# Norms, roundings and silu products moved to VectorE, the convolution's left tap split over ScalarE and GpSimd, and identity turns put into TensorE's queue

## Chip, cores and metric

One core of a Trainium2 chip. The metric is the device time of one execution in microseconds (us), the median of the runs shown; from run to run this kernel moves by under 1%.

## What is computed

Two layers over x of 2 examples x 512 tokens x 128 channels, with a context of 77 tokens per example. The reference, cut to what matters:

```python
# layer 0: cross attention in which the 512 tokens are the queries (8 heads of 64);
# its keys and values are the 512 tokens and the 77 context tokens together
q, k, v = heads(ln @ Wq), heads(kv @ Wk), heads(kv @ Wv)
x = x + tanh(g) * (softmax(q * 8 @ k.T) @ v) @ Wout
# layer 0: feed-forward on the layer norm of x, with quantised values and ternary weights
h = bit_linear(layernorm(x), w1)          # act_quant: round(x * 127 / max|x|) * max|x| / 127
h = silu(depthwise_conv1d(h, conv_w) + conv_b)     # three taps along the tokens, 512 channels
x = x + tanh(g) * bit_linear(h, w2)
# layer 1: attention to the 77 context tokens, 16 heads of 8, rotary factors on q and k
x = x + tanh(g) * attention(layernorm(x), ctx)
# layer 1: 8 experts of width 64, the two best per token, and a shared expert
y = x + tanh(g) * moe(layernorm(x))
```

## The kernel before, in words

Tokens lie on the 128 partitions in eight tiles, four for each example. The work is cut into items, each named by a kind and its indices, and each item passes several stages on several engines. The order in which every engine walks its items is written out by hand in the string PLAN, as words "kind:stage": F and B are TensorE's two visits, A1 and A2 ScalarE's, D0 to D3 VectorE's, P1 to P3 GpSimd's, Ca and Cd a copy out of PSUM by ScalarE or by VectorE; the number behind F is the PSUM bank that the item takes. Word by word the string is dealt out into one fixed list per engine, so each engine works strictly in its own list's order, and items meet through semaphores. An F item first waits until the former holder of its bank has been read out.

The kinds that matter, in the order in which one example passes them:

- x0, q, k, v: normalised and transposed input, projections. u: one tile and head of attention: scores (lines 596, 597), maximum on VectorE (1012), exponential on ScalarE (823), five transposes back (551, the helper `turn`), one copy of 640 columns (772 ScalarE, 774 VectorE). w: for a pair of heads, weighted sum of the values (615), 16 in all. o: output projection (622) and new X1 with the statistics of its norm.
- n: the norm ahead of the quantised layer, in halves of two tiles. VectorE gives mean and variance (950, 951, 961); GpSimd raises the variance to the power -1/2 (462) and normalises two tiles (465); VectorE finds their largest magnitudes (1224 to 1226); GpSimd rounds by adding and subtracting a large constant MAGIC (533, 536). f1 transposes the tiles.
- f2: per chunk of 128 channels, four chunks: product with the ternary weights in two passes (639, 640); ScalarE makes the middle tap and the bias (859), VectorE adds the left tap (1063) and the right tap (1065), ScalarE takes tanh (917); the silu product (tanh + 1) * y of chunks 0 and 1 is GpSimd's (488, 489), of chunks 2 and 3 VectorE's (1166). TH is the tanh buffer, two deep.
- f3: four transposes per tile (551), VectorE's largest magnitude (1071 to 1074), ScalarE scales and adds MAGIC (870), GpSimd subtracts it and writes bf16 (494). f4: transposes (652), ScalarE's copy (875), product (733), new X2 (1171) and the next norm, again by halves: power and normalisation on GpSimd.
- a1: transposes of the norm; a2: queries (667) and their rotation on VectorE (1107, 1110); a4: eight items per example, each scores of eight heads (675), maximum and subtraction on VectorE (1115, 1118), exponential (881), transposes, copy (786 or 788); a6: weighted sums (687, 692), reciprocal and product on VectorE (1124, 1125), output projection (746), and the norm by halves.
- m1, m3, m2, m4: transposes, router and shared expert (702, then a chain of small VectorE steps, 1130 to 1199), experts' two products (709, 751), tanh, mixture products on GpSimd (515, 543), and the last projection (757, 758) and store.

The second example's attention (u, w) is mixed with the first one's later layers; after its last w nothing is left that could fill the gaps but the first example's experts.

Of the kernel before, what the change touches and what calls it, by code (L numbers as in the profile page):

```python
# [100 lines left out]
x0:F0 x0:A1 k:F0 k:F2 x0:D2 k:A1 q:F4 k:A1 k:D1 v:F6 q:A1 k:D1 s:D2 q:F5 v:Ca q:D1 v:F2 q:A1 q:D1 u:F6 v:Ca  # L101
u:F0 u:F2 u:D1 u:D1 v:F5 u:A1 u:D1 u:A1 u:B v:Cd u:A1 u:B u:Cd u:B u:Ca u:F6 u:Ca u:F0 u:D1 u:F2 u:D1 u:A1
k:F4 u:D1 u:A1 u:B w:D0 k:A1 w:P1 u:B u:Cd u:A1 u:Cd u:F6 u:B k:D1 u:F0 u:Cd u:F4 u:D1 q:F2 u:D1 u:A1 q:F3
u:D1 u:A1 u:B u:A1 u:B w:D0 u:Cd q:A1 u:B u:Cd s:F6 w:F7 s:D1 k:F0 w:P1 u:Ca q:D1 w:A1 w:F6 k:A1 w:D1 k:D1
u:F0 w:A1 w:D1 u:F4 u:D1 u:F6 u:D1 g:F2 u:A1 u:D1 u:A1 u:B g:D1 u:A1 u:B u:Cd u:B u:Ca w:D0 w:P1 u:F0 u:Ca
u:F4 u:D1 u:F6 u:D1 u:A1 w:F2 u:D1 u:A1 u:A1 u:B w:A1 w:D1 u:B u:Ca u:B u:Cd u:F0 u:Ca k:F4 u:D1 q:A1 k:F6
u:A1 q:D1 k:A1 u:B k:A1 u:Cd k:F2 w:D0 k:D1 w:P1 k:F0 k:A1 k:D1 u:F4 k:D1 k:A1 u:F6 u:D1 w:F2 u:D1 u:A1 k:D1
u:A1 u:B w:A1 w:D1 u:B u:Ca u:F2 u:Cd u:F4 u:D1 u:F6 u:D1 a3:F0 u:A1 u:D1 u:A1 u:B u:A1 w:D0 a3:D1 w:P1 u:B
u:Ca u:B u:Ca u:F2 u:Ca w:F4 u:D1 a3:P1 u:A1 u:B w:A1 w:D1 u:F6 u:Ca u:F4 u:D1 u:F2 u:D1 u:A1 x0:F0 u:D1
u:A1 u:B u:A1 u:B w:D0 u:Cd w:P1 x0:A1 u:B u:Cd u:F6 u:Ca u:F4 u:D1 q:F2 u:D1 u:A1 u:F0 u:A1 u:B u:D1 q:A1  # L110
u:B u:Cd w:F3 u:A1 u:Cd w:D0 q:D1 u:F4 w:P1 w:A1 w:D1 u:F6 u:D1 u:B u:D1 k:F2 u:A1 u:Cd u:A1 u:B k:A1 u:B
u:Cd u:F0 u:Ca k:D1 u:F4 u:D1 w:F2 u:D1 u:A1 u:A1 w:D0 u:B w:A1 w:P1 w:D1 u:B u:Ca o:F2 u:Cd o:F3 o:D1 k:F4
# [37 lines left out]
def takes(item, stage):  # L150

    kind, n = item[0], item[-1]
    return {"x0 D2": n == 0, "f2 P1": n < HC // 2, "f2 D2": n >= HC // 2, "f4 P2": n % TP == TP - 1}.get(f"{kind} {stage}", True)


def orders():
# [3 lines left out]
    for word in PLAN.split():  # L160
        kind, stage = word.split(":")
        engine = COPIER.get(stage) or ENGINE[stage[0]]
        if stage[0] == "F":
            stage, bank = "F", int(stage[1:])
        elif stage[0] == "C":
            stage = "C"
# [1134 lines left out]
```

## Time and profile before

| what | us |
| --- | --- |
| median of 3 runs | 305.68 (303.73 to 306.17) |
| the profiled execution, its own time | 305.48 |
| its span, first to last instruction | 303.7 |
| TensorE busy | 267.9 |
| VectorE busy | 221.0 |
| ScalarE busy | 167.9 |
| GpSimd busy | 90.8 |

The profile is one execution. PE is TensorE's matmuls and transposes, PEld its weight loads (they overlap), DVE VectorE, ACT ScalarE, POOL GpSimd; "granted clock" 1.00 is 2.4 GHz and 0.50 is 1.2 GHz. Some 1.8 us of a run lie outside the span.

### The profile page before, as it was taken

The numbers are of one execution on the slowest core, as the hardware profiler recorded it, in microseconds if no ns is written. First come the engines' busy times: TensorE is split into PE (matmuls) and PEld (weight loads), VectorE is DVE, ScalarE is ACT, GpSimd is POOL, SyncE is SP. The second block draws the span as 40 slices with busy tenths as digits, with TensorE's granted clock in tenths as the row PEclk, the third lists the DMA queues.
The fourth block names the chain that finished last, engine by engine and source line by source line (L and its number), as shares of the span: only waits on it lengthen the run. The fifth ranks groups of instructions, "written<-read, shape, count | busy, mean of one in ns | idle before, by whom it ended". The sixth has DMA issues, their size and how long they took to land.

```text
span 303.7 us, 5371 instructions
## 1 busy us (share of the span) xinstructions
PE 267.9 (88%) x1806; PEld 191.1 (63%) x1806; DVE 221.0 (73%) x501; ACT 167.9 (55%) x336; POOL 90.8 (30%) x116
## 2 busy tenths in 40 slices
PE   0899999999999989978999999999779568997786
PEld 0568677698777665756766687775358444654455
DVE  3698976786867689949888984588687747665671
ACT  1385557677562589756757676452564612451451
POOL 2100000010005607346010030045996780003571
PEclk9999999999999999999999999999997965579899
DMA  7930000000000000000000000000000100000001
GB/s 214 370 108 3 0 1 2 0 2 0 3 0 2 1 0 0 2 3 1 0 3 0 2 0 2 1 2 0 2 1 9 29 0 0 0 2 0 0 3 35
DMA packets 5855, 6.12 MB, mean 20 GB/s; under 512 B 555, under 2 KB 4805, under 8 KB 5829
## 3 DMA queue, kind: packets, MB, share of 16 engines
q1 hardware_dynamic: 4944, 4.66, 4.9%
q10 hardware_dynamic: 885, 1.12, 1.0%
q8 instruction: 15, 0.25, 0.3%
q14 instruction: 11, 0.09, 0.1%
HBM read 5.26 MB, written 0.52 MB: 19 GB/s over the span
## 4 chain that ended last, share of the span: by engine, by line
PE 62%; DVE 17%; POOL 9%; issue 6%; ACT 4%; DMA 1%; DVEq 0%; ACTq 0%; POOLq 0%
PE slot L551 18%; PE slot L615 10%; PE slot L596 5%; POOL XN L465 5%; PE slot L597 4%; PE slot L757 3%; PE slot L675 3%; PE slot L587 3%; POOL vex L462 2%; PE slot L580 2%; PE slot L574 2%; PE slot L588 2%; PE slot L667 2%; DVE nm L1012 2%; DVE aq L1071 1%
## 5 line engine op out<-in xcount | busy, mean ns | idle before, releaser
L823 ACT ACTIVATE PR<-slot,nm 128x589 f32<-128x589 f32 x64 | 47.7, 751 | 22.2 <-DVE nm L1012 22.0
L1012 DVE TENSOR_REDUCE nm<-slot 128x1 f32<-128x589 f32 x64 | 46.3, 763 | 8.4 <-PE slot L597 8.1
L551 PE MATMUL slot<-K,PR 128*128 128x128 f32 (+1 forms) x320 | 44.2, 279 | 1.7 <-ACT PR L823 1.4
L551 PEld LDWEIGHTS slot<-K,PR 128*128 128x128 f32 (+1 forms) x320 | 35.4, 142 | 14.0 <-ACT PR L823 9.7
L596 PE MATMUL slot<-KH,Q 128*128 128x296 f32 (+1 forms) x128 | 40.8, 337 | 1.3 <-ACT PT L786 0.6
L615 PE MATMUL slot<-PT,V 128*64 128x256 f32 (+1 forms) x320 | 38.1, 384 | 0.0
L597 PE MATMUL slot<-KL,Q 128*128 128x296 f32 (+1 forms) x128 | 36.1, 299 | 0.0
L462 POOL TENSOR_TENSOR vex<-vex,mhalf 128x2 f32<-128x2 f32 (+1 forms) x14 | 10.7, 762 | 83.5 <-DVE vex L961 83.4
L482 POOL COPY REC<-rec 128x256 f32<-128x256 f32 x16 | 6.5, 408 | 95.7 <-DVE rec L990 59.6
L772 ACT ACTIVATE PT<-slot 128x640 f32<-128x640 f32 x36 | 25.1, 705 | 8.9 <-PE slot L551 6.0
L615 PEld LDWEIGHTS slot<-PT,V 128*64 128x64 f32 (+1 forms) x320 | 21.5, 137 | 11.9 <-issue 2.7
L596 PEld LDWEIGHTS slot<-KH,Q 128*128 128x128 f32 x128 | 24.1, 188 | 6.5 <-issue 1.5
L774 DVE COPY PT<-slot 128x640 f32<-128x640 f32 x28 | 22.5, 820 | 3.9 <-PE slot L551 3.7
L597 PEld LDWEIGHTS slot<-KL,Q 128*128 128x128 f32 x128 | 24.2, 189 | 0.7 <-issue 0.7
L551 PE MATMUL slot<-K,XN 128*128 128x128 f32 x32 | 8.5, 333 | 13.3 <-DVE XN L964 7.6
L465 POOL TENSOR_SCALAR XN<-X,mvx,vex 128x128 f32<-128x128 f32 x24 | 19.0, 798 | 1.3
L881 ACT ACTIVATE S<-S 128x616 f32<-128x616 f32 x16 | 11.3, 715 | 13.7 <-DVE S L1118 13.6
L1019 DVE TENSOR_TENSOR OT<-slot,RB 128x256 f32<-128x256 f32 x16 | 6.7, 421 | 14.7 <-ACT RB L835 12.8
L1115 DVE TENSOR_REDUCE mx<-slot 128x8 f32<-128x616 f32 x16 | 12.7, 796 | 6.2 <-PE slot L675 6.2
L551 PEld LDWEIGHTS slot<-K,XN 128*128 128x128 f32 x32 | 4.7, 153 | 18.3 <-issue 11.9
L551 PE MATMUL slot<-K,S 128*128 128x128 f32 x80 | 13.9, 325 | 2.3 <-ACT S L881 2.3
L551 PEld LDWEIGHTS slot<-K,S 128*128 128x128 f32 x80 | 10.9, 166 | 7.2 <-ACT S L881 4.7
(163 smaller groups left out, 539.0 us busy)
## 6 DMA issues: line engine op xcount, KB each, us to landing
CTT<-in_ctxT SPq DMA_DIRECT2D x1, 640.0 KB, 8.1
K<-in_const ACTq DMA_DIRECT2D x1, 589.0 KB, 8.3
WGU<-in_wgu SPq DMA_DIRECT2D x1, 580.0 KB, 8.7
X<-in_x SPq DMA_DIRECT2D x2, 256.0 KB, 3.9
WK<-in_wk SPq DMA_DIRECT2D x1, 512.0 KB, 6.2
out<-X SPq DMA_DIRECT2D x8, 64.0 KB, 1.5
L1W<-in_l1w SPq DMA_DIRECT2D x1, 384.0 KB, 8.1
WD<-in_wdT SPq DMA_DIRECT2D x1, 320.0 KB, 9.6
```

The source lines that it names most:

```text
L462: return pool.tensor_tensor(vex[:, n, r], vex[:, n, r], mhalf[:, r], ALU.pow)
L465: return pool.tensor_scalar(XN[:, m, :], src[:, m, :], mvx[:, n, m, 0:1], vex[:, n, m:m + 1], ALU.subtract, ALU.mult)
L551: return pe.transpose(dst, src, ident[0:p, 0:p])
L596: pe.matmul(W[:, K0 + lo:K0 + hi], q, KH[:, g % 4, lo:hi], start=True, stop=False)
L597: mm = pe.matmul(W[:, K0 + lo:K0 + hi], q, KL[:, g % 4, lo:hi], start=False, stop=True)
L615: mm = pe.matmul(W[e * DH0:(e + 1) * DH0, 0:N], V[0:r, c, h * DH0:(h + 1) * DH0], PT[0:r, s, c, e, :], start=(c == 0), stop=(c == 4))
L772: engine.activation(dst, src, ACT.Copy).then_inc(pt_copied["ACT"], 1)
L774: engine.tensor_copy(dst, src).then_inc(pt_copied["DVE"], 1)
L823: act.activation(PR[:, s, :], W[:, K0:K0 + KEYS0], ACT.Exp, bias=nm0[:, s:s + 1], accum_out=sum0[:, b, p * 2 + f, t, e:e + 1]).then_inc(pr ...
L881: act.activation(s1, s1, ACT.Exp, scale=float(DH1) ** -0.5).then_inc(exp1_ready, 1)
L1012: dve.tensor_reduce(nm0[:, s:s + 1], W[:, K0:K0 + KEYS0], AX.X, ALU.max, negate=True).then_inc(max_ready, 1)
L1115: link(dve.tensor_reduce(mx, w, AX.X, ALU.max))
```

## The change

Four edits and a new PLAN of 894 words instead of 874.

1. Normalisations of halves (n, f4, a6) and the rounding of n go from GpSimd to VectorE (stage D3); GpSimd keeps the power -1/2. The subtraction of MAGIC in f3 goes from GpSimd to ScalarE (6 of 8 tiles, Ca) or VectorE (2, Cd).
2. All eight silu products are VectorE's.
3. Convolution: ScalarE writes the left tap into TH (new stage A3), ScalarE the middle tap and VectorE the right tap as before, and GpSimd adds TH, moved by one column, to the sum. Then tanh overwrites TH.
4. A word such as "f3:F5+7" lets TensorE turn the identity 7 times into the item's slot after the slot is free and before it waits for its data; there are 54 such turns: 7 in x0's neighbour q at the start, 20 from f3 to f4, 12 in a2 and a4, 15 in m1, m3 and m4, the last three groups all in the second example.

In the new PLAN ScalarE takes 44 of 64 u copies (36 before), 14 of 16 a4 copies (15) and 4 of 6 v copies (5). In the last part the lists read, shortened:

```
VectorE before  w:16 a6 o:7 o:8 m2 n(half 4) m3 m2 m3 m2 f1 m2 a3 f2 f2 f2 f2 ... f3 x4 f4 x4 a2 a2 a4 x8
VectorE after   w:16 m2 m2 o:7 o:8 n(half 4) m2 m2 f1 a3 f2 m4 f2 f2 f2 m4 f2 m4 f2 ... f3 x4 f4 x2 norm f4 x2 a2 norm a4 a4 a2 a4 x6
TensorE before  f4 ... a1 a2 a1 a2 a4 a4 a4
TensorE after   f4 ... a1 a2(+2) a4(+8) a4 a4 a1 a2(+2)
```

```diff
-        return {... "f2 P1": n < HC // 2, "f2 D2": n >= HC // 2, "f4 P2": n % TP == TP - 1}
+        return {... "f4 P2": n % TP == TP - 1, "f4 D3": n % TP == TP - 1}
...
                 elif kind == "f2":
                     c = item[2]
-                    pool.wait_ge(tanh_done, n)
-                    th = TH[:, (n - 1) % 2, :]
-                    link_all([pool.tensor_scalar(th, th, 1.0, None, ALU.add)])
-                    pool.tensor_tensor(YC[:, c, :], YC[:, c, :], th, ALU.mult).then_inc(silu_by_pool, 1)
-                elif kind == "f3":
-                    pool.wait_ge(rounded, n)
-                    if n > 2:
-                        pool.wait_ge(qbt_ready, n - 2)
-                    pool.tensor_scalar(QB[:, (n - 1) % 2, :], QM[(n - 1) % 2], MAGIC, None,
-                                       ALU.subtract).then_inc(qb_ready, 1)
+                    pool.wait_ge(conv_left, n)
+                    pool.wait_ge(conv_right, n)
+                    pool.tensor_tensor(YC[:, c, 1:S], YC[:, c, 1:S], TH[:, (n - 1) % 2, 0:S - 1],
+                                       ALU.add).then_inc(conv_done, 1)
...
+                for _ in range(WARM[item]):
+                    turn(W[:, 0:P], ident)
...
+        def copy_quantised(engine, by, item):
+            n = upto(item)
+            engine.wait_ge(rounded, n)
+            if n > 2:
+                engine.wait_ge(qbt_ready, n - 2)
+            dst, src = QB[:, (n - 1) % 2, :], QM[(n - 1) % 2]
+            if by == "ACT":
+                engine.activation(dst, src, ACT.Copy, bias=-MAGIC).then_inc(qb_copied["ACT"], 1)
+            else:
+                engine.tensor_scalar(dst, src, MAGIC, None, ALU.subtract).then_inc(qb_copied["DVE"], 1)
...
+            def third(item):
+                c, n = item[2], upto(item)
+                act.wait_ge(front_done, NTH[item] + 1)
+                if n > 2:
+                    act.wait_ge(silu_ready, n - 2)
+                if item[1] == 1 and c < 2:
+                    act.wait_ge(hidw_ready, QT)
+                act.activation(TH[:, (n - 1) % 2, :], slot(item)[:, 0:S], ACT.Copy,
+                               scale=cw[:, 3 * c:3 * c + 1]).then_inc(conv_left, 1)
...
-                    link(dve.scalar_tensor_tensor(out=y[:, 1:S], in0=W[:, 0:S - 1], scalar=cw[:, 3 * c:3 * c + 1],
-                                                  in1=y[:, 1:S], op0=ALU.mult, op1=ALU.add))
...
             def third(item):
-                link(dve.tensor_reduce(aq[:, r, 0], XN[:, r, :], AX.X, ALU.max, apply_absolute_value=True))
-                link(dve.tensor_scalar(aq[:, r, 3], aq[:, r, 0], 1e-5, 1.0 / 127, ALU.max, ALU.mult))
-                dve.reciprocal(aq[:, r, 2], aq[:, r, 3]).then_inc(quant_ready, 1)
+                kind, n = item[0], upto(item)
+                if kind == "n":
+                    dve.wait_ge(rstd_ready[1], n)
+                    link_all([dve.tensor_scalar(XN[:, m, :], X1[:, m, :], mvx[:, 1, m, 0:1], vex[:, 1, m:m + 1],
+                                                ALU.subtract, ALU.mult) for m in tiles])
+                    link(dve.tensor_reduce(aq[:, r, 0], XN[:, r, :], AX.X, ALU.max, apply_absolute_value=True))
+                    link(dve.tensor_scalar(aq[:, r, 3], aq[:, r, 0], 1e-5, 1.0 / 127, ALU.max, ALU.mult))
+                    link(dve.reciprocal(aq[:, r, 2], aq[:, r, 3]))
+                    link_all([dve.tensor_scalar(XN[:, m, :], XN[:, m, :], aq[:, m, 2:3], MAGIC,
+                                                ALU.mult, ALU.add) for m in tiles])
+                    for m in tiles:
+                        dve.tensor_scalar(XN[:, m, :], XN[:, m, :], MAGIC, aq[:, m, 3:4],
+                                          ALU.subtract, ALU.mult).then_inc(xn_ready[1], 1)
+                elif kind == "f4":
+                    dve.wait_ge(rstd_ready[2], n // TP)
+                    for m in range(n - TP, n):
+                        normalise(2, X2, m, XN[:, m, :], xn_ready[2])
+                elif kind == "a6":
+                    dve.wait_ge(rstd_ready[3], n)
+                    for m in range(part_tiles(item).start, part_tiles(item).stop):
+                        normalise(3, X3, m, XN[:, m, :], xn_ready[3])
```

## Rows read from the trace of the kernel before

**Rows 1.** The page: busy time of the engines, and the granted clock by slice.
```profile
PE 267.9 (88%) x1806; PEld 191.1 (63%) x1806; DVE 221.0 (73%) x501; ACT 167.9 (55%) x336; POOL 90.8 (30%) x116
...
PEclk9999999999999999999999999999997965579899
```

**Rows 2.** Busy time by stretch: window, its length, then each engine, clock, DMA.
```profile
20.00:204.00 184.00, 176.19 (x1301) 132.31 (x1299) 142.98 (x283) 120.01 (x248) 38.05 (x53) 1.00 0.01 1
...
204.00:222.00 18.00, 15.85 (x86) 9.37 (x82) 13.81 (x48) 6.13 (x13) 13.83 (x19) 1.00 0.00 1
222.00:234.30 12.30, 10.00 (x53) 8.00 (x53) 9.83 (x20) 7.53 (x15) 10.25 (x9) 0.86 0.02 6
234.30:253.60 19.30, 13.41 (x87) 9.64 (x88) 11.69 (x40) 6.61 (x12) 11.84 (x12) 0.79 0.04 11
253.60:270.90 17.30, 15.71 (x97) 8.51 (x95) 12.47 (x16) 8.09 (x12) 0.00 (x0) 0.55 0.00 1
270.90:284.20 13.30, 11.19 (x91) 7.07 (x84) 8.10 (x26) 4.29 (x9) 2.29 (x3) 0.87 0.00 0
```

**Rows 3.** The same view in stretches of 2 us, where the clock fell.
```profile
226.00:228.00 2.00, 0.11 (x1) 0.12 (x2) 1.97 (x4) 1.58 (x4) 1.59 (x3) 1.00 0.00 0
...
244.00:246.00 2.00, 0.84 (x5) 0.41 (x5) 1.71 (x7) 0.26 (x1) 1.88 (x3) 0.85 0.00 0
```

**Rows 4.** Groups of instructions by line and shape: busy us, mean ns | idle before.
```profile
L772 ACT ACTIVATE PT<-slot 128x640 f32<-128x640 f32 x36 | 25.1, 705 | 8.9 <-PE slot L551 6.0 <-PE slot L615 2.5
...
L465 POOL TENSOR_SCALAR XN<-X,mvx,vex 128x128 f32<-128x128 f32 x24 | 19.0, 798 | 1.3
...
L494 POOL TENSOR_SCALAR QB<-W 128x512 bf16<-128x512 f32 x8 | 11.8, 1492 | 8.0 <-ACT W L870 6.1 <-ACT QBT L875 1.8
...
L859 ACT ACTIVATE YC<-slot,COL,cw 128x512 f32<-128x512 f32 x8 | 5.8, 786 | 0.5 <-PE slot L640 0.5
L536 POOL TENSOR_SCALAR XN<-XN,aq 128x128 f32<-128x128 f32 x8 | 5.7, 720 | 0.4
...
L917 ACT ACTIVATE TH<-YC 128x512 f32<-128x512 f32 x8 | 5.1, 642 | 2.9 <-POOL YC L489 2.1 <-DVE YC L1065 0.8
...
L533 POOL TENSOR_SCALAR XN<-XN,aq 128x128 f32<-128x128 f32 x8 | 2.9, 371 | 2.9 <-DVE aq L1226 2.9
...
L964 DVE TENSOR_SCALAR XN<-X,mvx,vex 128x128 f32<-128x128 f32 x8 | 2.2, 342 | 1.5 <-POOL vex L462 1.5
...
L852 ACT ACTIVATE XH<-slot 128x512 fp32r<-128x512 f32 x2 | 1.2, 598 | 2.2 <-PE slot L551 2.2
```

**Rows 5.** Instructions in order of time, 234 to 282 us: start, us, instruction.
```profile
234.45 1.96 PE L551 MATMUL slot<-K,YC 128*128 128x128 f32 x16
...
237.17 5.97 POOL L494 TENSOR_SCALAR QB<-W 128x512 bf16<-128x512 f32 x4 [4.34 <-ACT W L870]
...
243.43 0.17 DVE L961 TENSOR_SCALAR vex<-mvx 128x2 f32<-128x2 f32 x1
...
250.16 2.04 PE L667 MATMUL slot<-LT,L1W 128*128 128x256 f32 x4 [0.52 <-ACT LT L877]
...
253.58 0.80 DVE L1115 TENSOR_REDUCE mx<-slot 128x8 f32<-128x616 f32 x1
254.41 0.80 DVE L1118 TENSOR_TENSOR S<-slot,mx 128x616 f32<-128x616 f32 x1
...
279.92 1.91 PE L709 MATMUL slot<-WGU,LT 128*128 128x512 f32 x2
...
281.62 1.06 PE L746 MATMUL slot<-L1W,A1T 128*128 128x128 f32 x4
```

**Rows 6.** In order of time around 215 us: a GpSimd product beside a VectorE step.
```profile
215.31 1.27 POOL L543 TENSOR_TENSOR HM<-HM,TH 128x512 f32<-128x512 f32 x1
...
215.84 0.77 DVE L1225 TENSOR_SCALAR aq<-aq 128x2 f32<-128x2 f32 x1
```

**Rows 7.** Busy time by stretch, in the first example's convolution.
```profile
110.00:120.00 10.00, 9.80 (x45) 6.27 (x45) 9.78 (x14) 9.95 (x20) 5.54 (x4) 1.00 0.00 0
```

More of the change, by code:

```diff
@@ L163, in orders @@
         if stage[0] == "F":
-            stage, bank = "F", int(stage[1:])
+            bank, turns = [int(n) for n in (stage[1:] + "+0").split("+")[:2]]
+            stage = "F"
         elif stage[0] == "C":
@@ L173, in orders @@
             mine = range(bank, bank + 1 + wide(item))
-            bank_of[item], had[item] = bank, list(dict.fromkeys(holder[i] for i in mine if i in holder))
+            bank_of[item], warm[item], had[item] = bank, turns, list(dict.fromkeys(holder[i] for i in mine if i in holder))
             holder.update({i: item for i in mine})
-    return order, bank_of, had, copier
-ORDER, BANK_OF, HAD, COPIES = orders()
+    return order, bank_of, had, copier, warm
+ORDER, BANK_OF, HAD, COPIES, WARM = orders()
 NTH = {x: n for n, x in enumerate(x for x, stage in ORDER["PE"] if stage == "F")}
@@ L402, in col, with quantised @@
             return COL[:, COLS.index(name):COLS.index(name) + 1]
-        def silu(item):
-            _, b, c = item
-            half = HC // 2
-            return (silu_by_pool, b * half + c + 1) if c < half else (silu_by_dve, b * half + c - half + 1)
+        def quantised(n):
+            item = KINDS["f3"][n - 1]
+            return qb_copied[COPIES[item]], copied(item, COPIES[item])
         def half_pair(item):
@@ L647, in front @@
                     n = upto(item)
-                    pe.wait_ge(qb_ready, n)
+                    pe.wait_ge(*quantised(n))
                     pe.wait_ge(identb_ready, 1)
@@ L868, in first @@
                     if n > 2:
[L869 removed]
+                        act.wait_ge(*quantised(n - 2))
                     act.activation(QM[(n - 1) % 2], W[:, 0:HID], ACT.Identity, bias=COL[:, NCOL - 1:NCOL],
@@ L921, in second @@
                     if n % QT == 1:
-                        for c in range(HC):
-                            act.wait_ge(*silu(("f2", item[1], c)))
+                        act.wait_ge(silu_ready, HC * (n // QT + 1))
                     if n > 2:
@@ L926, in second @@
                     act.activation(HB[:, (n - 1) % 2, :], slot(item)[:, 0:MH], ACT.Tanh, scale=0.5).then_inc(gate_tanh, 1)
+            def third(item):
[7 more added lines that the diff above has]
+                               scale=cw[:, 3 * c:3 * c + 1]).then_inc(conv_left, 1)
             def copy(item):
-                {"u": copy_turned, "a4": copy_turned1, "v": copy_values}[item[0]](act, "ACT", item)
-            walk("ACT", {"A1": first, "A2": second, "C": copy})
+                {"u": copy_turned, "a4": copy_turned1, "v": copy_values, "f3": copy_quantised}[item[0]](act, "ACT", item)
+            walk("ACT", {"A1": first, "A2": second, "A3": third, "C": copy})
         @block.vector
```

175 lines of the change are left out of this document (72 added, 103 removed).

## The prediction

> **What bounds the kernel now.** I read the page's busy line and slices first: TensorE is busy for 88% of the span, and its granted clock sinks only in the last third [rows 1]. So I cut the span at the places where the work changes, with a view that gives busy time by stretch [rows 2]. From 20 to 204 us, where attention of both examples runs with the later layers of the first one between, TensorE is busy 176.2 of 184 us at full clock. VectorE has 143 there, ScalarE 120, GpSimd 38. That stretch is near TensorE's, and at most 7.8 us of visible idle can go from it. From 204 us on, the last 100 us, no engine is full in most stretches: the second example's quantised layer, its second attention and its experts form one chain of short steps. What a step is worth is read from there, and that is where nearly all my terms lie.
>
> In that tail the clock falls from 2.4 to 1.2 GHz. It fell at 228 us, after 226 to 228 in which TensorE was busy for 0.11 us, and again inside 244 to 246, after a stretch of short turns with gaps [rows 3]. It then stayed down through nearly all of 253.6 to 270.9 (mean 0.55) although TensorE was busy 15.7 of 17.3 us there [rows 2]. So in that stretch TensorE is the bound only because of its clock.
>
> **The change, part by part**, against the profiled execution (305.48 us, span 303.7; the median of the runs is 0.2 above).
>
> Prices of the moved operations [rows 4]. A normalisation of a tile costs 0.80 us on GpSimd and 0.34 on VectorE; a half of two tiles takes 1.60 or 0.68. The second rounding step costs 0.72 a tile on GpSimd and on VectorE the same 0.34, since it has the same form. Subtracting the magic number from 512 columns costs 1.49 on GpSimd; no row shows it elsewhere. ScalarE's nearest row is a plain 512-column copy, 0.60, and the one with scale and bias from a tensor is 0.79; I take 0.60 to 0.70. The left tap on ScalarE lies between the same two rows; I take 0.70. GpSimd's sum of two 512-column operands has the form of its product, 1.27 [rows 6]. A turn of the identity is a turn like the 16 that took 1.96 us [rows 5], 0.12 each: 54 of them are 6.6 us of TensorE, 47 of them in the tail, all placed after the slot is free and before the wait for data. While TensorE would wait anyway they cost nothing; uncovered, all would cost 6.6.
>
> *20 to 204 us: -1.0.* GpSimd's latencies in the first example's quantised layer go, which should close about 2 of the 7.8 us idle. The new order puts a transposed half and a router product (0.9 us) ahead of the last weighted sum. The bounds are -5 and +5, since an order of 894 words is new throughout.
>
> *204 to 222 us (end of attention to the quantised layer): -2.0.* GpSimd is busy 13.8 of 18 us [rows 2]. The second half's normalisation gives 0.9, its rounding (now 0.68 + 0.68 for 2.17) 0.8. The power no longer queues behind another half's normalisation (0.5), and the second attention's reciprocal of the first example is out of the way of the last head pair (0.8). That is 3.0. Against it stands the following. A VectorE step on 128x2 elements took 0.77 us at 215.84 instead of 0.32 and ended when GpSimd's 1.27 us product, begun at 215.31, ended [rows 6]. The new tensor_scalars are of that kind, and the mixture products still run on GpSimd beside them: I charge 1.0, with 0 and 2.5 as ends.
>
> The Trainium skill has this as a rule (SBUF — State Buffer, "Who interferes with whom"): a VectorE tensor_scalar in a two-port mode, or one with two SBUF inputs against a reading GpSimd, is blocked until the other engine's instruction ends. The trace agrees in that one pair of rows. It speaks against the change in just this place: by it each of the three linked groups of a half could be blocked once.
>
> *222 to 234.3 us (convolution and silu): +1.2.* Before, GpSimd was busy for 10.25 of the 12.3 us, with half of the silu products and the last mixture products. The new chain for a chunk is longer: left tap, middle tap, right tap, GpSimd sum 1.27, tanh, product. ScalarE now does 4 x (0.70 + 0.79 + 0.64) = 8.5 us [rows 4] and all four expert outputs' copies, some 3.4, where it was busy 7.5 of 12.3 [rows 2]; it is near full. Since TH has two buffers, the third left tap waits for the first product. Followed, the last product ends 13.4 us after the first convolution product, where it was 12.2.
>
> *234.3 to 253.6 us (quantise, second linear layer, first queries): -4.3.* Before, GpSimd's four subtractions fill 237.17 to 243.14 [rows 5]. In their place ScalarE does 4 x 0.78 rounding, 3 x 0.6 subtraction and 4 x 0.60 copies, 7.3 us from about the same start, so the second half's variance hardly moves. But the first half's, at 243.43 before [rows 5], comes about 1.5 earlier, its normalisation is 0.9 shorter, and its query product runs at full clock (-1.0). The new order also puts the scores of three tiles ahead of the second half's queries, which began at 250.16 and took 2.04 at half clock [rows 5]: -2.3. The turns back after it and one normalisation ahead on VectorE take 0.6 back. That is -5.1, and I leave 0.8 for hand-overs I have not followed.
>
> *253.6 to 270.9 us (scores of the second attention): -2.3.* At full clock VectorE bounds it: 8 tiles x 2 x 0.80, the maximum and the subtraction, of which the first tile's maximum is at 253.58 [rows 5] = 12.8, plus the second half's rotation of 1.3 now inside, plus hand-overs: 15.0 instead of 17.3. This rests on the clock, which the turns hold only if they stand in the right gaps.
>
> *270.9 to 284.2 us: -2.7.* The output projection ran at 281.62 behind an expert product of 1.91 us at half clock [rows 5]; its input was ready at 279.3. At full clock and ahead of that product it goes at once.
>
> *284.2 to 303.7 us: 0.* The last normalisation is 0.9 shorter, but VectorE now does 2 us of router steps ahead of it, which earlier ran beside GpSimd's normalisation. GpSimd's eight mixture products stay. The turns stand ahead of waits.
>
> Sum: -1.0 - 2.0 + 1.2 - 4.3 - 2.3 - 2.7 = -11.1, so 305.5 - 11.1 = **294.4 us**.
>
> **The rivals.** A difference of about 1% (3 us) is what a measurement of this kernel tells from none.
> - *The clock falls all the same* around the quantisation. For it: a short gap with 0.11 us of work was enough at 228, and even 90% busy in the score stretch did not bring it back for long [rows 2, 3]. Against it: 20 turns stand between quantisation and the first transposes and 12 more up to the scores. Then the -2.3 goes, the query products take 1.0 and their neighbours 0.8 back, and the projection 1.2: 305.5 - 11.1 + 5.3 = 299.7. Chance 0.20.
>   The Trainium skill (TensorE: Matmul & The Clock Gate, "What's actually happening") says that the slow state is the default and activity releases it. By that alone the score stretch at 91% busy should have come back early, and this rival would cost little; the row at 0.55 says otherwise, and I go by the row.
> - *VectorE is blocked by GpSimd at each step.* For it rows 6; against it, GpSimd loses half of its work. Three blocks of 1.27 between the last weighted sum and the quantised layer, one more in the last router chain, less the 1.0 charged, are +4.1: 298.5. Chance 0.14.
> - *ScalarE becomes the bound in the attention stretch, and the kernel gets slower.* It takes 8 more copies of transposed scores (0.70 each [rows 4], 5.6), 8 left taps (5.6) and 6 subtractions (3.6): 14.8 us in all. For it: from 110 to 120 us it is already busy 9.95 of 10 [rows 7], and score tiles wait for its exponential. Against it: over the whole stretch it has 120 of 184 us, and would have some 130. It decides from the point at which ScalarE is full while heads wait. Were every added microsecond on the path and nothing won in the first 204 us, 305.5 - 10.1 + 14.8 = 310. Chance 0.07.
> - *The new order is also tighter in attention*: 5 of the 7.8 us idle go, 290.4. Chance 0.16.
> - *The turns do not hold anything but cost their time*: 6.6 us uncovered, 301.0 with the rest as forecast. Chance 0.05.
>
> **How the numbers follow.** The forecast has 0.38. Range: 288.5 (the tighter order with a little more) to 302.5 (the clock's rival with 2.8 for order). Faster by over 1%, that is under 302.6: 0.36 of the forecast's share, 0.17 of the clock's, 0.12 of the blocking's, 0.16 and 0.03 of the last two, together 0.84. Within 1%: 0.09. Slower: 0.07.
>
> **What would show each step.** Granted clock 1.0 from 204 us to the end confirms the turns; any stretch at 0.5 between quantisation and the last score tile is the rival. The eight score tiles should follow each other on VectorE 1.6 us apart. VectorE's tensor_scalars on 128x128 should have a mean near 0.34; one near 0.8 or above means blocking. The last silu product should come some 13 us after the first convolution product. The attention stretch should end within 3 us of before. The prediction is wrong if the last weighted sum comes over 5 us later than 204.5 us, or if the score stretch keeps its 17 us at full clock.

## The result, and the profile after

The changed kernel takes **296.0 us** (median of 4 runs, 295.1 to 297.0) against 305.75 before: ratio 0.971, 95% interval 0.966 to 0.977. The forecast was 294.4 in a range of 288.5 to 302.5. The profiled execution took 296.25 us (span 294.5), 9.2 less than the profiled one of before, where the sum had 11.1.

The page's busy line and clock by slice, as in [rows 1]:

```profile
PE 264.3 (90%) x1860; PEld 194.5 (66%) x1860; DVE 225.4 (77%) x533; ACT 180.0 (61%) x356; POOL 50.3 (17%) x68
...
PEclk9999999999999999999999999999989799999799
```

GpSimd lost 40 us of work, yet VectorE has only 4 more: what it got from GpSimd (norms, roundings, half of the silu products, two subtractions) is mostly paid by the eight left taps and eight copies of transposed scores that it gave away. TensorE made 54 operations more in 3.6 us less, because its clock was higher. It did not stay up, though: three slices are below 9.

I cut the span at seven events that every kernel has: the start of the last weighted sum, the first convolution-layer product of the second example, the end of its last silu product, the first maximum and the last subtraction of its second attention's scores, the last variance, and the end. Busy time of the changed kernel between them, with the columns of [rows 2]:

```profile
20.00:202.00 182.00, 176.91 (x1314) 134.08 (x1312) 147.12 (x316) 128.97 (x262) 18.36 (x30) 1.00 0.01 1
202.00:219.60 17.60, 14.40 (x79) 9.28 (x79) 14.18 (x40) 5.92 (x12) 9.78 (x9) 0.97 0.01 1
219.60:233.20 13.60, 11.68 (x69) 9.86 (x69) 8.49 (x19) 10.36 (x20) 5.75 (x5) 0.88 0.05 15
233.20:247.70 14.50, 10.72 (x87) 8.71 (x87) 11.55 (x39) 7.12 (x12) 2.80 (x4) 0.92 0.02 6
247.70:261.50 13.80, 10.64 (x103) 6.22 (x102) 12.63 (x18) 8.44 (x13) 0.00 (x0) 1.00 0.01 1
261.50:272.50 11.00, 10.20 (x98) 6.21 (x87) 8.97 (x27) 4.38 (x10) 0.71 (x1) 1.00 0.01 1
272.50:294.50 22.00, 17.36 (x89) 11.68 (x87) 9.87 (x35) 7.24 (x18) 9.77 (x9) 0.90 0.04 13
```

The same cuts in both kernels, from their timelines, beside the terms of the prediction:

| stretch | before | after | difference | predicted |
| --- | --- | --- | --- | --- |
| start to last weighted sum | 204.5 | 202.0 | -2.5 | -1.0 |
| to the convolution | 17.6 | 17.6 | +0.1 | -2.0 |
| convolution and silu | 12.2 | 13.6 | +1.4 | +1.2 |
| quantise to the first maximum | 19.3 | 14.5 | -4.8 | -4.3 |
| scores of the second attention | 16.5 | 13.8 | -2.7 | -2.3 |
| to the last variance | 13.9 | 11.0 | -3.0 | -2.7 |
| to the end | 19.7 | 22.0 | +2.3 | 0 |

Four terms are within 0.5 us and the first is 1.5 off, inside its bounds. Two failed: the stretch ahead of the convolution gave nothing, and the last one lost 2.3.

Groups of the changed kernel by line and shape, as in [rows 4]:

```profile
L909 ACT ACTIVATE TH<-slot,cw 128x512 f32<-128x512 f32 x8 | 5.5, 688 | 0.3 <-DVE YC L1148 0.2
...
L777 ACT ACTIVATE QB<-W 128x512 bf16<-128x512 f32 x6 | 3.7, 626 | 0.1
...
L779 DVE TENSOR_SCALAR QB<-W 128x512 bf16<-128x512 f32 x2 | 0.9, 427 | 0.1
...
L474 POOL TENSOR_TENSOR YC<-YC,TH 128x511 f32<-128x511 f32 x8 | 10.1, 1270 | 14.0 <-DVE YC L1047 14.0
...
L948 DVE TENSOR_SCALAR XN<-X,mvx,vex 128x128 f32<-128x128 f32 x24 | 8.5, 404 | 3.6 <-POOL vex L452 3.1 <-DVE cwt L1181 0.5
...
L1207 DVE TENSOR_SCALAR XN<-X,mvx,vex 128x128 f32<-128x128 f32 x8 | 3.9, 529 | 1.6 <-POOL vex L452 1.5
...
L515 PE MATMUL slot<-K 128*128 128x128 f32 x54 | 9.6, 310 | 0.0
```

The prices bounded from neighbouring rows hold: left tap 0.69 (0.70 taken), subtraction 0.63 (0.60 to 0.70), GpSimd's sum 1.27. A rounding step, taken at 0.34 a tile, is cheaper: 0.48 for two tiles. The normalisation of one tile, 0.34 in [rows 4], has means of 0.53 and 0.40. The timeline shows why, first at the last half ahead of the quantised layer, then at the last norm of the second attention (start, us, instruction, wait and its releaser):

```profile
212.23 2.04 POOL L495 TENSOR_TENSOR HM<-HM,cwt 128x512 f32<-128x512 f32 x2
212.30 2.06 DVE L1207 TENSOR_SCALAR XN<-X,mvx,vex 128x128 f32<-128x128 f32 x2 [0.81 <-POOL vex L452]
...
216.91 0.66 PE L515 MATMUL slot<-K,XN 128*128 128x128 f32 x4 [2.09 <-DVE TH L1125]
...
274.93 1.70 DVE L948 TENSOR_SCALAR XN<-X,mvx,vex 128x128 f32<-128x128 f32 x2 [0.50 <-DVE cwt L1181]
```

A pair beside an idle GpSimd takes 0.60. Here one took 2.06. The same moments with each instruction by itself:

```profile
212.23 1.04 POOL L495 TENSOR_TENSOR HM<-HM,cwt 128x512 f32<-128x512 f32 x1
212.30 1.06 DVE L1207 TENSOR_SCALAR XN<-X,mvx,vex 128x128 f32<-128x128 f32 x1 [0.81 <-POOL vex L452]
...
213.23 1.04 POOL L495 TENSOR_TENSOR HM<-HM,cwt 128x512 f32<-128x512 f32 x1
213.28 1.08 DVE L1207 TENSOR_SCALAR XN<-X,mvx,vex 128x128 f32<-128x128 f32 x1
```

Each of the two normalisations began just behind a mixture product of GpSimd and ended 0.09 us after it (213.36 after 213.27, 214.36 after 214.27), so each waited for one product. The pair at 274.93 (0.70 and 1.08) stood in the same way beside two products begun at 274.51. Two single steps of VectorE were held earlier in the stretch ahead of the convolution, both 0.17 when free:

```profile
203.10 0.60 DVE L1210 TENSOR_SCALAR aq<-aq 128x2 f32<-128x2 f32 x1
...
206.33 0.96 DVE L1179 SCALAR_TENSOR_TENSOR cwt<-lg,hot 128x16 f32<-128x16 f32 x1
```

With the pair's 1.5 us that is 2.7 us of blocking in this stretch, where 1.0 was charged.

Last, the clock, in stretches of 2 us around its three falls:

```profile
214.00:216.00 2.00, 0.81 (x8) 0.54 (x5) 1.83 (x8) 0.36 (x1) 0.27 (x1) 1.00 0.00 0
216.00:218.00 2.00, 1.09 (x8) 0.92 (x9) 1.45 (x4) 0.40 (x1) 1.07 (x1) 1.00 0.00 0
218.00:220.00 2.00, 2.00 (x13) 2.00 (x13) 0.69 (x1) 0.19 (x1) 1.43 (x2) 0.62 0.00 0
...
228.00:230.00 2.00, 0.32 (x2) 0.12 (x2) 1.34 (x3) 2.00 (x5) 0.68 (x1) 1.00 0.11 33
...
232.00:234.00 2.00, 2.00 (x12) 2.00 (x11) 1.24 (x3) 0.49 (x1) 0.00 (x0) 0.54 0.11 33
...
274.00:276.00 2.00, 0.71 (x5) 0.30 (x3) 1.43 (x5) 0.27 (x1) 1.49 (x2) 1.00 0.02 4
276.00:278.00 2.00, 1.28 (x5) 0.87 (x5) 1.83 (x3) 0.38 (x1) 1.25 (x2) 0.63 0.00 0
278.00:280.00 2.00, 2.00 (x6) 1.38 (x6) 0.94 (x9) 0.00 (x0) 1.79 (x2) 0.52 0.00 0
```

Each fall to 1.2 GHz comes after TensorE had little to do: ahead of 218, from 228 to 230, and from 274 to 276. The first and the third of these gaps stand right behind the two blocked normalisations. From 236 to 276, where before the clock was down for most of the time, it is at 1.00.

### The profile page after: what moved, and what is told of

The parts are those of the page before. It is cut to its first block and busy times, and to the rows that moved or that the text cites. A ratio compares the mean times of both kernels' runs of the same rounds, so it can differ in the third digit from the quotient of the medians.

```text
span 294.5 us, 5492 instructions
## 1 busy us (share of the span) xinstructions
PE 264.3 (90%) x1860; PEld 194.5 (66%) x1860; DVE 225.4 (77%) x533; ACT 180.0 (61%) x356; POOL 50.3 (17%) x68
## 5 line engine op out<-in xcount | busy, mean ns | idle before, releaser
L801 ACT ACTIVATE PR<-slot,nm 128x589 f32<-128x589 f32 x64 | 47.6, 749 | 15.3 <-DVE nm L996 14.9
L515 PEld LDWEIGHTS slot<-K,PR 128*128 128x128 f32 (+1 forms) x320 | 35.7, 142 | 12.9 <-ACT PR L801 8.6
L738 ACT ACTIVATE PT<-slot 128x640 f32<-128x640 f32 x44 | 29.8, 705 | 11.7 <-PE slot L515 11.2
L581 PEld LDWEIGHTS slot<-PT,V 128*64 128x64 f32 (+1 forms) x320 | 21.6, 137 | 11.9 <-issue 2.7
L452 POOL TENSOR_TENSOR vex<-vex,mhalf 128x2 f32<-128x2 f32 (+1 forms) x14 | 10.4, 745 | 82.6 <-DVE vex L945 82.6
L740 DVE COPY PT<-slot 128x640 f32<-128x640 f32 x20 | 16.4, 822 | 4.5 <-PE slot L515 4.2
L515 PE MATMUL slot<-K,XN 128*128 128x128 f32 x32 | 7.0, 315 | 12.2 <-DVE XN L948 10.0
L1003 DVE TENSOR_TENSOR OT<-slot,RB 128x256 f32<-128x256 f32 x16 | 6.7, 421 | 13.2 <-ACT RB L813 12.8
L515 PE MATMUL slot<-K,S 128*128 128x128 f32 x80 | 11.5, 281 | 3.2 <-ACT S L859 3.0
L515 PEld LDWEIGHTS slot<-K,XN 128*128 128x128 f32 x32 | 4.3, 147 | 14.8 <-issue 9.5
L515 PEld LDWEIGHTS slot<-K,S 128*128 128x128 f32 x80 | 8.6, 141 | 7.4 <-ACT S L859 6.5
L1100 DVE TENSOR_TENSOR S<-slot,mx 128x616 f32<-128x616 f32 x16 | 12.8, 799 | 0.6
```

Source lines behind the costliest of these rows:

```text
L452: pool.tensor_tensor(vex[:, n, r], vex[:, n, r], mhalf[:, r], ALU.pow).then_inc(rstd_ready[n], 1)
L515: return pe.transpose(dst, src, ident[0:p, 0:p])
L581: mm = pe.matmul(W[e * DH0:(e + 1) * DH0, 0:N], V[0:r, c, h * DH0:(h + 1) * DH0], PT[0:r, s, c, e, :], start=(c == 0), stop=(c == 4))
L738: engine.activation(dst, src, ACT.Copy).then_inc(pt_copied["ACT"], 1)
L740: engine.tensor_copy(dst, src).then_inc(pt_copied["DVE"], 1)
L801: act.activation(PR[:, s, :], W[:, K0:K0 + KEYS0], ACT.Exp, bias=nm0[:, s:s + 1], accum_out=sum0[:, b, p * 2 + f, t, e:e + 1]).then_inc(pr ...
```

## Experiments

Each kernel is the changed one with the edit shown, unless it says otherwise. Times are medians; ratios are against the kernel before in the same comparison, with their 95% intervals. The stages of their traces stand in one table at the end of this section.

### One part taken back at a time

**No turns.**

```diff
-                for _ in range(WARM[item]):
+                for _ in range(0):
```

> The changed kernel with its 54 identity turns left out, everything else the same (296.0 us changed, 305.7 before). My theory: the turns hold the granted clock at 2.4 GHz from quantisation to the last score tile; without them it falls there, the score stretch (first maximum to last subtraction, 13.8 us with turns) goes back to 16 us or more, and the run is 299 to 302 us. Rival: the new order is dense enough by itself, and the turns only cost; then 295 to 296.5 us with the clock at 1.00 over the score stretch.

Measured 301.1 us, ratio 0.988 (0.982 to 0.994), granted clock 0.943. Its stretches from the last silu product to the first maximum, and on to the last subtraction:

```profile
232.90:248.80 15.90, 11.53 (x61) 8.30 (x63) 11.21 (x39) 7.13 (x12) 2.81 (x4) 0.50 0.02 5
248.80:263.90 15.10, 12.70 (x102) 7.74 (x101) 12.85 (x19) 8.44 (x13) 0.00 (x0) 0.79 0.00 1
```

At 0.50 all the way through the quantised second layer and 0.79 in the scores, where the changed kernel has 0.92 and 1.00. The medians differ by 5.1 us, the two profiled executions by 4.0: 1.4 and 1.2 of these are there, and 1.7 in the last stretch. So the turns cost less than they give.

**The turns alone**, in the kernel before: the same numbers behind the same items.

```diff
 # kernel before
+                for _ in range(WARM[item]):
+                    turn(W[:, 0:P], ident)
...
-f3:F2 ... f4:F2 ... a4:F4 ...
+f3:F2+7 ... f4:F2+7 ... a4:F4+8 ...
```

> The kernel before with only the 54 identity turns added, at the same items as in the changed kernel. My theory: they hold the clock in the old order too, so queries and scores run at 2.4 GHz and 3 to 5 us go: 301 to 303 us. Rival: the turns work only in the new order, since in the old one the gaps lie elsewhere: 305 to 307 us, with the clock at 0.5 over most of the score stretch.

Measured 302.7 us, ratio 0.996 (0.991 to 1.000), clock 0.972. The kernel before had a median of 305.2 us beside it: 2.5 less, at the edge of what can be told. The turns raise the clock in the old order too (0.91 in its quantise stage, 0.66 in its scores), but bring half as much. The quantise stage gets no shorter (19.7 us); that GpSimd's four subtractions, which still stand there, are what ends it is my reading, not tested here.

**Norms and roundings back on GpSimd.**

```diff
-dve.tensor_scalar(XN[:, m, :], ..., ALU.subtract, ALU.mult)
+pool.tensor_scalar(XN[:, m, :], ..., ALU.subtract, ALU.mult)
```

> The changed kernel with the normalisations of halves and the rounding back on GpSimd (order otherwise the same). My theory: each link on the chain of the tail is 0.8 to 1.0 us longer, four of them, but the two blocks of VectorE behind GpSimd's mixture products (1.5 and 1.1 us) go with it: 297 to 299 us. Rival 1, the move of the norms is most of the gain: 301 us or more. Rival 2, the blocking eats all of what the move gives: 295 to 296.5 us.

Measured 300.0 us, ratio 0.983 (0.975 to 0.990), between the theory's 299 and rival 1's 301. The moves of the norms are worth 4.0 us, but not where I put them. In the stretch up to the convolution the kernel with GpSimd's norms is 0.8 *faster* (16.8 against 17.6). It loses 2.7 before the last weighted sum and 2.7 between quantisation and the first maximum.

**Left tap back on VectorE.**

```diff
+                    link(dve.scalar_tensor_tensor(out=YC[:, c, 1:S], in0=W[:, 0:S - 1], scalar=cw[:, 3 * c:3 * c + 1],
+                                                  in1=YC[:, c, 1:S], op0=ALU.mult, op1=ALU.add))
-f2:A3 ... f2:P1
```

> The changed kernel with the left tap back on VectorE as one more instruction of 0.75 us per chunk, without ScalarE's left tap and GpSimd's sum. My theory: the convolution stretch of the second example (first product to first transpose after it, 14.0 us) is longer only because of the longer chain per chunk, and goes back to 12 to 13 us; the run is 294 to 295.5 us. Rival: VectorE is what the split relieves, above all in the first example's layer beside attention; then the run is 297 us or more.

Measured 295.35 us, ratio 0.967 (0.961 to 0.974): the same as the changed kernel, or slightly better. The convolution takes 12.4 us instead of 13.6, so the +1.2 of the prediction is that edit. Yet only 0.65 of it reaches the total, which is within the spread of the runs (293.8 to 296.7).

**Subtraction back on GpSimd.**

```diff
-                engine.activation(dst, src, ACT.Copy, bias=-MAGIC).then_inc(qb_copied["ACT"], 1)
+                pool.tensor_scalar(dst, src, MAGIC, None, ALU.subtract).then_inc(qb_copied["POOL"], 1)
-f3:Ca f3:Cd
+f3:Cp
```

> The changed kernel with the subtraction of the magic number in f3 back on GpSimd (1.49 us a tile instead of 0.63 on ScalarE or 0.43 on VectorE). My theory: last silu product to first maximum of the second attention, 14.5 us, grows by 1 to 2 us, since the first half's two tiles pass through GpSimd one after the other; the run is 297 to 298 us. Rival 1: ScalarE, now relieved, was what bound the stretch, and nothing is lost (295.5 to 296.5). Rival 2: this was the main gain: 300 us or more.

Measured 299.6 us, ratio 0.983 (0.976 to 0.989): the move is worth 3.6 us, more than my theory had and just short of rival 2. In its trace the first example's part is 2.2 later at the last weighted sum and the quantise stage is 2.4 longer. Four subtractions of 1.47 us stand in a row again:

```profile
237.58 2.95 POOL L514 TENSOR_SCALAR QB<-W 128x512 bf16<-128x512 f32 x2 [4.97 <-ACT W L855]
...
240.92 2.94 POOL L514 TENSOR_SCALAR QB<-W 128x512 bf16<-128x512 f32 x2 [0.38 <-ACT W L855]
```

### The moves and the order, each without the other

**The moves in the old order**, no turns (norms, roundings, silu products and subtraction as in the changed kernel, left tap on VectorE).

```diff
 # changed code, PLAN of the kernel before, with
-n:P3        f3:P1       f2:P1 (silu)
+(in n:D3)   f3:Ca/Cd    f2:D2         f4:D3 a6:D3
```

> The old order of words with the new assignment of norms, rounding, silu products and subtractions, without the split of the left tap and without identity turns. My theory: of the changed kernel's 9.7 us the moves alone give a third to a half, since the links are shorter but the order of the score stretch, the second half's queries and the clock stay as they were: 300.5 to 303 us. Rival 1: the moves are all of it: 299 us or less. Rival 2: without the new order the moved work collides on VectorE with the rest: 305 us or more.

Measured 305.4 us, ratio 0.998 (0.994 to 1.002): nothing, as rival 2 had it. This holds for the places in the old list at which I put the moved stages; others were not tried. The stretch ahead of the convolution is 20.5 us, 3 more than before, and three pairs of normalisations in the tail are blocked (2.29 us at 215.29, 1.42 at 248.74, 1.31 at 285.47).

**The order alone**: the new PLAN with the old assignment, no turns.

```diff
 # PLAN of the changed kernel, with
-f3:Ca f3:Cd   f2:D2 (chunks 0 and 1)   f4:D3 a6:D3   n:D3        +7 +2 ...
+f3:Cp         f2:P1                                  n:D3 n:P3
```

> The changed kernel's order of work with none of its other parts: the norms, the roundings, the subtraction and half the silu products are back on GpSimd, both taps on VectorE, no turns. Theory (the order is worth something only with the assignment it was fitted to, as the moves in the old order gave 305.4 against 305.8): 304 to 308 us, no better than the kernel before. Rival (the new order is the gain, the moves and turns are small): 299 to 302 us. In the theory each part needs the other, and order and moves together are worth the 4.4 us by which the kernel without turns (301.1) beats the one before (305.2).

Measured 307.9 us, ratio 1.011 (1.006 to 1.017): 2.6 us *slower*. Its last weighted sum begins 3.4 us later than before. (Its profiled execution, 305.6 us, is the fastest of four, so the table below shows less of the loss than the median.) So neither the moves nor the order gains by itself; together, with the split tap and without turns, they give 301.1, that is 4.1 less, and the turns add 5.1.

### Two places where the prediction failed

**The mixture's third product waits** until the last half of the norm is through, so that GpSimd is idle beside it.

```diff
                     m = n - 1
+                    if n == 3:
+                        pool.wait_ge(xn_ready[1], NT)
                     pool.wait_ge(weights_ready, m // TP + 1)
```

> The changed kernel with one wait more: GpSimd's mixture product of the first example's third tile waits until the second example's norm and rounding are done, so no GpSimd instruction stands beside them. My theory: the two normalisations that took 2.06 us behind two mixture products take 0.60, and the first convolution product comes 1 to 1.5 us earlier after the last weighted sum (17.6 us now): 294.5 to 295 us. Rival: the transposes of the norm wait anyway, for the PSUM bank that the expert step of the third tile holds; then that stretch changes by less than 0.5 us.

Measured 295.8 us, ratio 0.968 (0.959 to 0.978), from 292.8 to 297.0. The pair of normalisations now takes the short time:

```profile
212.02 0.60 DVE L1209 TENSOR_SCALAR XN<-X,mvx,vex 128x128 f32<-128x128 f32 x2 [0.81 <-POOL vex L452]
```

and the stretch is 15.6 us instead of 17.6. But the convolution takes 14.8 instead of 13.6, and the median is the same. Part of that 1.2 is a wait that has nothing to do with the clock. ScalarE's left tap writes TH, which the held mixture products still read:

```profile
219.24 0.69 ACT L911 ACTIVATE TH<-slot,cw 128x512 f32<-128x512 f32 x1 [0.79 <-POOL HM L510]
```

It comes 1.9 us after the first convolution product, where the changed kernel has 1.2 (220.88 after 219.64). Behind it one of VectorE's silu products, at 223.88, is held by GpSimd's sum and takes 1.14 us instead of 0.68.

```profile
226.00:228.00 2.00, 0.69 (x5) 0.37 (x3) 1.31 (x4) 2.00 (x4) 0.52 (x1) 1.00 0.11 33
228.00:230.00 2.00, 1.60 (x7) 1.60 (x8) 1.13 (x2) 0.97 (x3) 1.98 (x2) 0.51 0.11 33
```

The gap of TensorE in the convolution is still there as well, 2 us earlier, with ScalarE full (2.00 of 2.00), and the clock falls behind it.

**The last norm ahead of the router.**

```diff
-m3:D2 a6:P2 m2:B m2:A1 m2:A2 a6:D3
+a6:D3 m3:D2 a6:P2 m2:B m2:A1 m2:A2
```

> The changed kernel with VectorE's normalisation of the very last half put ahead of the router chain of the half before, no other change. My theory: the last stretch (last variance to the end, 22.0 us, 19.7 before) is longer because this normalisation stands behind 1.8 us of router steps and then behind two mixture products (1.70 us instead of 0.60); so it shrinks by 1 to 2 us: 294 to 295 us. Rival: the router chain comes later by as much, and the mixture products of the two tiles on GpSimd are what the end waits for; then no change (under 0.5 us).

Measured 296.9 us, ratio 0.974 (0.968 to 0.980), above the theory's range. The last stretch is 20.3 us instead of 22.0, the local gain expected, but the total is no lower. In this execution the clock fell in the score stretch (0.82 and 0.75 in two stretches of 4 us from 255 to 263), which the edit does not touch, and the stretch took 15.0 us instead of 13.8. So one profile of a kernel whose clock falls now here, now there does not tell a gain of 1 us.

### The edits together

**All three edits**: left tap on VectorE, the mixture's wait, the norm ahead of the router.

> The changed kernel with the left tap back on VectorE, the third product of the mixture held on GpSimd until the last norm of attention, and the last norm of the second attention put ahead of the router. One by one these gave 295.4, 295.8 and 296.9 us against 296.0. Theory (VectorE's work sets each stage, but what one edit saves is waited for again at the next point where another engine is late): 293.5 to 296 us, no more than 1% below the changed kernel. Rival (the savings add, 0.7 from the tap, 2.0 before the second convolution and 1.8 in the last stretch): 291 to 292.5 us, a version that beats both.

Measured **290.9 us**, ratio 0.954 (0.950 to 0.958), five runs of six between 290.5 and 291.0. The rival was right, and even its lower end was passed: one by one the edits gave -0.65, -0.2 and +0.9, together -5.1. These are differences from the changed kernel's 296.0, which was not run again beside them; against the kernel before in the same series, whose median moved between 305.2 and 305.8, they are -0.1, -0.3 and +0.8, together -4.6.

```profile
PEclk9999999999999999999999999999999999999999
```
```profile
202.20:217.80 15.60, 13.85 (x79) 8.72 (x79) 12.72 (x40) 5.90 (x12) 8.02 (x8) 1.00 0.01 2
217.80:230.00 12.20, 10.88 (x71) 8.46 (x69) 10.85 (x23) 7.76 (x16) 2.49 (x3) 1.00 0.06 17
```

The clock does not fall at all, and each stretch has its short form: 15.6 us from the wait and 12.2 from the tap. The five runs have a granted clock of 1.00; the sixth has 0.977 and took 294.9 us. Within this one kernel 4.0 us go with the falls. That is one run, without a trace, so where its clock fell is not known.

**Tap and wait only**, the norm behind the router again.

> The kernel with three edits less one: the last norm stands behind the router again, the left tap on VectorE and the wait before the mixture's third product stay. The three edits together gave 290.9 us in five of six runs, each with TensorE at 1.00 throughout, and 294.9 in the sixth, at 0.977. Theory (the savings are kept as soon as no gap of TensorE is long enough for its clock to fall, and one of the three edits closes each gap): the gap near 274 in the last stretch comes back and the clock falls behind it, 292 to 294 us, granted clock 0.98 to 0.99 with 1.00 up to 270. Rival (the clock in the last stretch is not what the norm's place changes, the gain came from the two edits ahead of the second convolution): 290.5 to 291.5 us. Second rival (the edits' VectorE time itself is the gain, the clock is not): also the range of the theory, but with the falls before 240 still in the windows.

Measured 292.0 us, ratio 0.956 (0.951 to 0.961). Two of its runs have a clock of 0.998 and 0.999 (291.1 and 291.5 us), two have 0.982 (292.6 and 292.8). The profiled one is of the former: the last norm is blocked (2.05 us) and TensorE has a gap, and the clock held all the same:

```profile
270.00:272.00 2.00, 0.64 (x6) 0.40 (x4) 1.71 (x6) 0.51 (x1) 0.98 (x1) 1.00 0.01 4
272.00:274.00 2.00, 0.88 (x5) 0.45 (x5) 2.00 (x4) 0.39 (x1) 1.24 (x3) 1.00 0.00 0
```

The time stands at the edge between theory and rival, and the truth is between them: tap and wait bring 4.0 of the 5.1 us. The norm's place brings 0.7 in the last stretch of the profile, and perhaps fewer falls: five of six runs at 1.00 with it, two of four close to 1.00 without. So few runs do not decide it.

**The three edits without turns.**

> The kernel with three edits, without its 54 turns of the identity. Theory (the turns still carry the clock over the gaps of the score and attention stretches, where TensorE is busy about 60% of the time): 294.5 to 297 us with a granted clock of 0.94 to 0.96, as much slower as the changed kernel without turns was (301.1 against 296.0). Rival (with the gaps ahead of the convolution gone the clock holds by itself, so the turns are no longer needed): 290.5 to 292 us at 0.99 to 1.00.

Measured 297.1 us, ratio 0.972 (0.968 to 0.977), clock 0.965 (0.959 in one run): the theory. The turns are worth 6.2 us here. Up to 230 us the clock holds without them; it falls in the quantisation (0.66 from 230.3 to 245.9) and is at 0.79 in the scores.

### The stages of all kernels

From one profiled execution each, us; the first column is the start of the last weighted sum.

| kernel | last w | to conv. | conv. | quantise | scores | to var. | to end |
| --- | --- | --- | --- | --- | --- | --- | --- |
| before | 204.5 | 17.6 | 12.2 | 19.3 | 16.5 | 13.9 | 19.7 |
| changed | 202.0 | 17.6 | 13.6 | 14.5 | 13.8 | 11.0 | 22.0 |
| no turns | 201.5 | 18.1 | 13.4 | 15.9 | 15.0 | 11.0 | 23.7 |
| turns alone | 205.2 | 17.6 | 12.2 | 19.7 | 15.1 | 12.9 | 19.6 |
| norms on GpSimd | 204.7 | 16.8 | 14.3 | 17.2 | 13.8 | 11.9 | 19.4 |
| left tap on VectorE | 202.5 | 18.3 | 12.4 | 14.8 | 13.8 | 11.0 | 21.0 |
| subtraction on GpSimd | 204.2 | 17.1 | 12.8 | 16.9 | 13.8 | 11.0 | 20.7 |
| old order | 205.1 | 20.5 | 10.3 | 18.8 | 16.6 | 12.2 | 21.0 |
| order alone | 207.9 | 16.8 | 12.8 | 17.6 | 15.5 | 13.6 | 19.4 |
| mixture waits | 201.7 | 15.6 | 14.8 | 15.3 | 13.8 | 11.0 | 20.7 |
| norm first | 201.1 | 18.5 | 13.6 | 14.8 | 15.0 | 11.0 | 20.3 |
| three edits | 202.2 | 15.6 | 12.2 | 14.1 | 13.8 | 11.0 | 20.3 |
| tap and wait | 202.0 | 15.6 | 12.2 | 14.1 | 13.8 | 11.0 | 21.0 |
| three, no turns | 202.4 | 15.6 | 12.2 | 15.7 | 15.1 | 11.0 | 23.0 |

## Why the prediction was right, point by point

The total was right to 1.6 us, and four of seven terms to 0.5. It was right because the large terms lie in the quantisation and behind it. The missing 1.9 us of the profiled sum are two failed terms (+2.1 and +2.3) against gains elsewhere (-2.5, of which 1.5 before the last weighted sum). That these cancel by half is luck.

- *20 to 204 us, -1.0, measured -2.5*: inside its bounds. Taking back the norms or the subtraction loses 2.7 and 2.2 us there, so GpSimd's latencies in the first example's quantised layer were what the moves took away, as the prediction said; the order alone made this part 3.4 longer.
- *204 to 222 us, -2.0, measured +0.1*: the step that failed. "I charge 1.0, with 0 and 2.5 as ends" was too small. The second half's normalisation of two tiles was blocked for 1.5 us. It then held VectorE's next task, which empties the PSUM slot that the transposes of f1 wait for (2.09 us at 216.91, though the normalised tile was there at 216.25). With the one cause taken away (mixture waits) the stretch is 2.0 shorter. That puts it 2.0 below the kernel before, where the gains without the charge were summed to 3.0, so those were too large as well. The last variance of this norm comes 9.3 us after the start of the last weighted sum (211.32 after 202.00), before it was 7.8 (212.31 after 204.49). In between stands VectorE's product for the last pair of heads. It comes 5.7 us after that start (207.74), where it came after 3.6 (208.12): VectorE now does the first half's norm and rounding and the router steps of the first example ahead of it, and two of these steps are blocked (0.4 and 0.8 us). Ahead of the variance 1.5 us were thus lost, a term that the prediction does not have; behind it 1.4 were won, and 3.4 without the blocked pair. How much of the 1.5 is VectorE's new work, how much the order and how much the two blocks was not separated.
  The Trainium skill says it as the trace does (SBUF — State Buffer, "Who interferes with whom"): the engine that issues second is fully blocked for the other's whole instruction. The rows agree, instruction by instruction: two normalisations, two products, two waits. The prediction's free time for the step of [rows 6], 0.32 us, is a mean that has the blocked step in it; the other three took 0.17, so that step alone had lost 0.60.
- *Convolution, +1.2, measured +1.4*: right in size and cause. ScalarE was busy 10.4 of 13.6 us. Putting the tap back takes 1.2 off (13.6 to 12.4), and from the kernel in which the mixture waits it takes 2.6 off (14.8 to 12.2), since ScalarE then no longer writes TH ahead of tanh and GpSimd has no sum beside VectorE's products. The split of the left tap is the one part of the change whose own stretch got longer.
- *Quantise to first maximum, -4.3, measured -4.8*, *scores, -2.3, measured -2.7*, *to the last variance, -2.7, measured -3.0*: right. The two causes can be told apart. With GpSimd's subtraction the first of them is 2.4 longer, with its norms 2.7; without turns it is 1.4 longer. In the scores only the clock counts: 13.8 us in every kernel in the new order whose turns held the clock there, 15.0 to 15.5 where it was down (the three kernels without turns, and norm first).
- *The end, 0, measured +2.3*: "The turns stand ahead of waits" did not do here. The last norm stands behind the router chain, is blocked for 1.1 us, and TensorE was busy 0.71 of 2 us from 274 to 276. The clock then fell. Only 7 turns stand there. They run from 273.47 to 274.40, and their item then waits for the norm until 275.69.

**The rivals.** *The clock falls all the same* was placed in the quantisation, and there it was wrong: no fall begins among its 20 and 12 turns, and the one that begins at 232 is over before 236. It fell in three other places, of which two stand behind blocked normalisations. "Granted clock 1.0 from 204 us to the end" was thus not met (0.88 to 0.97 in four of six stretches, 0.981 over the span), and is what the kernel with three edits reaches. *VectorE is blocked* came largely true: four of its steps ahead of the convolution lost 2.7 us where it has three blocks of 1.27, and the last pair lost 1.1. *ScalarE becomes the bound*: not in attention, only in the convolution. *Tighter order in attention*: half of it came. *Turns uncovered*: refuted by the kernels without turns, 5.1 and 6.2 us slower.

**Why the edits add up only together.** With the tap alone the gap ahead of the convolution stays (TensorE busy 0.64 us from 216 to 218), and the clock falls to 0.57 behind it. With the wait alone the gap inside the convolution stays, and it falls to 0.51 there. With both neither fall is seen. These are one profiled execution of each kernel, and a gap does not always bring a fall: TensorE had 0.64 us of work in 2 with tap and wait (270 to 272) and kept its clock. What each fall costs by itself was not measured. In the kernel with the tap there was one more fall, at 238 us, after 2 us in which TensorE was busy for 1.03. The kernel with three edits had 0.92 from 234 to 236, soon after the same point of its quantisation, and did not fall; what decides between these is open. The clock is not the only reason either. In the convolution the tap saves 1.2, the wait loses 1.2, and both together save 1.4: there the tap takes away what made the wait lose, ScalarE's write to TH behind the held mixture products and GpSimd's sum that held VectorE. The table has these 1.4 us; how the rest divides was not measured.

## What to carry to other kernels

Moving work from GpSimd to VectorE pays less where GpSimd's other work runs beside it: hold back what is not urgent there (one wait, 2.0 us in its stretch), and look at what the held work then stands in front of. Turns of the identity ahead of a wait are cheap and were worth 5 to 6 us in a tail of short steps; give each wait as many as it is long, and look in the profile for every stretch below 1.00. When single edits seem to give nothing although their own stretch gets shorter, look for the next fall of the clock or the next shared buffer and try them together: -0.65, -0.2 and +0.9 became -5.1.

## What was not expected of the hardware

- Two VectorE normalisations behind two GpSimd products of 1.04 us waited one product each (2.06 instead of 0.60 us), so a row of GpSimd instructions can hold a row of VectorE's step by step. Steps of 128x16 elements wait as long: in the kernel with three edits, where the norm itself is free, a router step of 0.17 met the first of two products of 1.27 us:

```profile
274.34 2.54 POOL L509 TENSOR_TENSOR HM<-HM,TH 128x512 f32<-128x512 f32 x2
...
274.59 1.05 DVE L1125 TENSOR_TENSOR lg<-lg,top 128x16 f32<-128x16 f32 x1
```

- Much of the spread from run to run goes with TensorE's clock. In the kernel with three edits 1.00 goes with 290.5 to 291.0 us and 0.977 with 294.9; in the one in which the mixture waits 292.75 and 294.7 us both go with 0.988, 296.85 and 297.0 with 0.977. The 2 us between the first two are not explained by it. The mean clock differs between executions of one kernel, so whether a gap brings a fall does too.
- ScalarE writes 512 columns with a scale per partition in 0.69 us and with a fixed bias to bf16 in 0.63, a little above its plain copy of 0.60 [rows 4].
